# Two more products of constants per chunk in the relation passes of a graph network

## The reference, cut to what matters

```python
# second layer
t = jnp.einsum('nd,rdo->rno', h, weight)
msg = t[etype, src]
agg = jax.ops.segment_sum(msg, dst, num_segments=h.shape[0])
return jax.nn.relu(agg + bias)
# fourth layer
xt = jnp.einsum('ni,rio->rno', x, weight)
messages = xt[edge_type, col]
out = jax.ops.segment_sum(messages, row, num_segments=num_nodes)
return jax.nn.relu(out + bias)
```

## Time and profile before

| | us |
|---|---|
| median of 3 runs | 8551.53 (8549.6 to 8559.96) |
| the profiled execution | 8619.9 |
| first relation pass, 4015 to 5206 | 1191 |
| second relation pass, 7417 to 8582 | 1165 |
| PE busy over the whole execution | 4852.2 (56%) |
| POOL busy over the whole execution | 5243.4 (61%) |
| DVE busy over the whole execution | 3573.0 (41%) |

### The profile page before, as it was taken

One profiled execution on the slowest core, in us unless ns is written; L12 is line 12 of the kernel. 1 busy time (PEld: TensorE's weight loads), 2 busy tenths in 40 slices (PEclk: granted clock), 3 DMA queues, 4 the chain that ended last, 5 costly groups with the idle time before them and its releaser, 6 DMA issues. The chain is left out here.

```text
span 8619.9 us, 69117 instructions
## 1 busy us (share of the span) xinstructions
PE 4852.2 (56%) x17004; PEld 2990.1 (35%) x17004; DVE 3573.0 (41%) x9196; ACT 1730.7 (20%) x7055; POOL 5243.4 (61%) x5610
## 2 busy tenths in 40 slices
PE   3202235555557777777455543777777876655554
PEld 1100014444435555543333332222223663333332
DVE  4201014333335555564222224444445776244445
ACT  0000001111123333322000002222223874000000
POOL 5577756666666666632666662666665882366665
PEclk6655557777778888888666666878888998866666
DMA  3001012222235555554333335656666884333333
GB/s 96 2 3 39 15 40 90 90 89 89 91 116 176 177 175 175 177 114 156 92 93 93 92 93 67 186 184 187 187 187 177 267 271 156 117 93 92 91 94 85
DMA packets 422550, 1037.69 MB, mean 120 GB/s; under 512 B 159993, under 2 KB 188189, under 8 KB 415516
## 3 DMA queue, kind: packets, MB, share of 16 engines
q0 software_dynamic: 223616, 552.46, 22.9%
q1 hardware_dynamic: 198556, 480.95, 17.4%
HBM read 716.74 MB, written 316.30 MB: 120 GB/s over the span
## 5 line engine op out<-in xcount | busy, mean ns | idle before, releaser
L944 POOL DMA_INDIRECT rel_rows<-relation_rows,rel_ring_row x1640 | 1558.3, 950 | 1177.7 <-ACT rel_ring_end L937 695.1
L956 PE MATMUL rel_sums<-rel_rows,rel_hot 128*128 128x256 f32 x3280 | 1197.1, 509 | 1178.3 <-issue 448.5
L956 PEld LDWEIGHTS rel_sums<-rel_rows,rel_hot 128*128 128x128 f32 x3280 | 785.7, 252 | 1590.1 <-issue 1076.9
L982 DVE TENSOR_TENSOR g_acc<-rel_sums,g_acc 128x256 f32 x1224 | 517.8, 423 | 1532.9 <-DMA records_by_dst<-g_big 548.5
L1913 POOL DMA_INDIRECT nmax_rows<-messages,nmax_ring_row x832 | 788.6, 948 | 566.3 <-ACT nmax_ring_row L1869 327.6
L761 POOL DMA_INDIRECT rows_by_src<-spread_rows,spread_ring_place x832 | 803.2, 965 | 483.8 <-issue 254.3
L838 POOL DMA_INDIRECT both_rows<-batch_normed,both_ring_row x832 | 791.0, 951 | 460.9 <-ACT both_ring_end L807 231.3
L605 POOL DMA_INDIRECT records_by_dst<-sort_ring_rec,sort_ring_place x784 | 810.4, 1034 | 390.6 <-issue 241.2
L739 PE MATMUL spread_p_r<-g_big,spread_hot_t 128*128 x1664 | 631.5, 545 | 542.0 <-ACT spread_hot_t L674 358.8
L1961 DVE TENSOR_TENSOR g_big<-nmax_short,g_big 128x512 f32 x832 | 575.7, 692 | 659.9 <-PE nmax_short L1934 288.6
L1934 PE MATMUL nmax_short<-nmax_rows,g_ident_b 128*128 128x512 bf16 x2496 | 800.3, 436 | 0.0
(11 more groups left out here) (443 smaller groups left out, 6114.8 us busy)
## 6 DMA issues: line engine op xcount, KB each, us to landing
kept_rows<-nmax_rows SPq DMA_DIRECT2D x208, 536.0 KB
g_big<-kept_rows SPq DMA_DIRECT2D x208, 536.0 KB
both_out_rows<-rows_by_src SPq DMA_DIRECT2D x202, 520.0 KB
att_local_row<-local_of_edge SPq DMA_DIRECT2D x52, 512.0 KB
rel_rows<-relation_rows,rel_ring_row POOLq DMA_INDIRECT x1640
relation_rows<-mix_table SPq DMA_DIRECT2D x25, 1024.0 KB
relation_rows<-fin_table SPq DMA_DIRECT2D x25, 1024.0 KB, 3.9
rows_by_src<-spread_rows,spread_ring_place POOLq DMA_INDIRECT x832
```

Source lines behind the costliest of these rows:

```text
L944: pool.indirect_dma_start(rows[:, j, 0:words], None, table, bass.IndirectOffsetOnAxis(ap=ring_row[:, j:j + 1], axis=0)).then_inc(landed[n ...
L956: last = nc.tensor.matmul(sums[:, unit % slots, 0:width], hot[:, j, :], rows[:, j, :], start=of == 0, stop=of == GRAIN[k] - 1)
L982: nc.vector.tensor_tensor(at, sums[:, unit % slots, 0:width], at, ALU.add).then_inc(added, 1)
```

## The change

Behind each chunk's product PE computes two products of the constant `g.earlier` with itself, repeated four times to 512 columns, both bf16. They go to a PSUM bank of their own, `unused`, which nothing reads. To make room, `sums` gets 14 slots in seven banks instead of 16 in eight. The signal `summed` stays with the product of the group's fourth chunk.

```diff
-    ahead, slots = ring - 2, 16
+    ahead, slots, fills = ring - 2, 14, 2
...
-        sums = m.ps("sums", [P, slots, 8 * 512 // slots])
+        sums = m.ps("sums", [P, slots, 7 * 512 // slots])
+        unused = m.ps("unused", [P, GRP, P])
...
                     last = nc.tensor.matmul(sums[:, unit % slots, 0:width], hot[:, j, :], rows[:, j, :],
                                             start=of == 0, stop=of == GRAIN[k] - 1)
-                last.then_inc(summed, 1)
+                    if q == GRP - 1:
+                        last.then_inc(summed, 1)
+                    for _ in range(fills):
+                        nc.tensor.matmul(unused[:], g.earlier[:], g.earlier[:].unsqueeze(1).broadcast_to([P, GRP, P]),
+                                         start=True, stop=True)
```

## The result

The changed kernel takes 8597.99 us (median of 4 runs, 8592.52 to 8601.66) against 8553.39 for the kernel before (4 runs): ratio 1.0049, interval 1.0038 to 1.0061. It is slower by 45 us. The forecast was 354 us slower, so the sign and the place were right and the size was wrong by a factor of eight. The profiled execution takes 8599.9 us.

A forecast was written before the change was run, and what follows sets the result against it. The prediction took POOL's gathers, held up now and then waiting for ACT, as the bound. More stops (+350) and the signal's place (+4) made 354 on 8551.5, about 8905 us; own range 8740 to 9055, with rivals 8540 to 9420.

The forecast's parts named there:

- What bounds the kernel: Both relation passes: POOL's gathers, 1.254 us a chunk, plus 131 and 137 us of stops set the end; PE has room.
- The release in records: End of a late stretch: PE holds some 64 unsignalled loads and matmuls, so a release frees two groups instead of four.
- Cycles: From one POOL stop to the next: 4 groups, 16 chunks, so 52 and 50.5 stops instead of 23.4 and 24.5.
- The stop stays 5.6 us: POOL's stop at the end of each cycle keeps its length of 5.6 us net though stops come more often.
- the term of +306 to +387 us: Both passes: added POOL stops from twice the records, +306 with 4 groups a cycle, +387 with 3.5; 350 taken.
- The signal's place: End of each pass: summed has six fills of its group ahead of it, about 2 us per pass, +4 in all.
- One PSUM bank less: PE against DVE with 14 slots instead of 16: nothing taken; about +9 us if slots still bind.
- the hidden case: Rival, both passes: as many groups freed per stop as now, ring hides most; 0 to +90 us, 8550 to 8640; chance 0.22.
- PE bound by records: Rival, both passes: a late stretch comes each 160 records, 1.96 us a chunk, about 9410 us; chance 0.15.
- The faster case: Rival, both passes: fills shorten PE's idle time, signals stay prompt, POOL's stops return; 8285 to 8530 us; chance 0.13.

The follow-up runs named there:

- slots14_c: The kernel before with 14 PSUM slots instead of 16 and no fills, in conditions where POOL stops: ratio 1.0008 (0.9998 to 1.0018).
- pace2: The kernel before with a 128x300 write by POOL ahead of each gather, each waiting for the last, in conditions with stops: ratio 1.0136 (1.0119 to 1.0153).
- fill3: The changed kernel with three fills of 512 columns per chunk instead of two, in conditions with stops: ratio 1.0092 to the kernel before (1.0075 to 1.0109).
- change_again: The changed kernel as it is, run once more in conditions where POOL never stops: ratio 1.0004 to the kernel before (0.9995 to 1.0014).
- slots14_b: The kernel before with 14 PSUM slots instead of 16 and no fills, in conditions where POOL never stops: ratio 0.9999 (0.9989 to 1.0008).

## Why the prediction was wrong, step by step

- **What bounds the kernel: right, as far as it went.** POOL's gathers and its stops make up the pass, and PE has room: without stops 175 us of PE's time went into a pass and none showed, with stops 564 went into both passes and 45 showed. What the prediction did not see is that something other than POOL sets 1.42 us a chunk, which the stops only make up for.
- **The release in records: right for the change, but 64 is not a fixed number.** A release frees two groups with two fills, long or short, and one with six short ones, 64 loads and matmuls each. But it is 80 with three fills (two groups of 40), 48 in the second pass of slots14_c (three groups of 16), and in the first pass of before three of the 18 releases have a fifth group 0.23 us behind the fourth. In that second pass PE has a PSUM slot for each chunk, and four groups are just the 16 slots of before, three what fits in 14; so there the slots explain the release as well as the records. That PE holds a count of 64, as the prediction reads it, is not shown.
- **Cycles: nearly right, with some luck.** Forecast were 16 chunks and some 52 and 50 stops; measured were mostly 20 and mostly 16 chunks, and 43 and 53 stops (gaps of more than 1.6 us from one gather's start to the next). The way there was not sound: by the same count before had 33 and 26 stops and not the 23.4 and 24.5 from which the forecast set out.
- **The stop stays 5.6 us: this step failed,** and the prediction had named that as a sign of being wrong. In the cycles shown it is 3.1 to 3.8 us with two fills, 3.1 with three, 2.0 to 2.8 with six short ones. 5.6 / 32, 3.8 / 20, 3.1 / 16 and (2.0 + 2.8) / 20 are 0.175, 0.19, 0.19 and 0.24 us a chunk. I took the stop for a price that each cycle pays, and it is what POOL had run ahead since the last one: 1.42 less 1.25 us for each chunk, which is 0.17. Twice as many stops are then half as long, and the term of +306 to +387 us comes to +24 by the two profiles and to 33 to 39 by kernels in equal conditions. slots14_c (cycles of 28, stops of 4.9) and pace2 (no stop, and 117 us where step and stops make 390) show the same without fills. What sets the 1.42 us stays open. The rows had a warning: the earlier trace rows has 41 waits inside the first pass, 3.5 us each on the mean, and the earlier trace rows a stop of 4413.98 - 4407.93 - 1.25 = 4.8 us there and 5.6 in the second pass, and yet both passes came to 1.42 us a chunk. I divided the sum of the stops by 5.6 to get 23.4 of them, and so put in what I should have tested.
- **The signal's place: small, as forecast,** +4 in the sum. The ends of the passes grew by 8 and 6 us in the profile, but the second end was 25.6 us long in slots14_c, too, so the size of this part isn't shown.
- **One PSUM bank less: right in the time,** 1.0008 and 0.9999 for the slots alone. The slots do shorten the cycles of the second pass by one group where there are no fills; it costs nothing, as the stops shrink with them.
- **The rivals.** The time lies in the middle of the range of the hidden case, 8550 to 8640. The mechanism of that rival (as many groups freed as before) is not what happened: two are freed, and it costs little for another reason. PE bound by records wanted 1.96 us a chunk and fell with the change's own 1.437, and with the 1.448 of fill3. The faster case fell: fills do shorten PE's idle time and raise the clock, from 0.67 to 0.80, and from 0.76 to 0.98 in change_again, but the late stretches stayed where there were any, and the time did not fall. The Trainium skill, page "TensorE: Matmul & The Clock Gate", section "Why this matters for your kernels", advises to keep TensorE busy without gaps. The traces agree that the clock follows; the time does not, as PE doesn't set the pace of these passes.

## What to carry to other kernels

A producer that runs ahead and then stops may have a slower pace behind it, and the stops are only the balance: divide the whole stage by its steps before pricing one stop, and compare two stages whose stops have different lengths. Idle time of an engine that doesn't set the pace is nearly free (here the fills kept PE busy for 0.21 to 0.34 us more a chunk), and filling it for the sake of the clock is worth nothing unless that engine sets the pace. To test for such a floor, slow the producer on purpose: if the kernel loses less than the added time, something else was setting the pace.

## What the runs showed of the hardware

- The same kernel takes 8553 to 8610 us or 7627 to 7637, without a change in it. Nearly all of the difference lies in the six stages in which POOL issues indirect DMAs: in the profile of before they take 1123, 1237, 1250, 1182, 1225 and 1150 us from the first gather or scatter to the last, in that of slots14_b 1014, 1053, 1041, 1041, 1039 and 1012, together 967 of the 994 us between these two profiles. POOL's own step is the same in both (1.254 and 1.251 us in the passes).
- In the slower conditions there is a floor of 1.42 us for a chunk of 128 gathered rows. It held in kernels with 4 to 10 loads and matmuls a chunk within some 2% (1.418 to 1.448 us), whether POOL stopped 26 or 100 times a pass. It shows itself on other engines: PE starts an instruction per 1.40 us in late stretches and one per 0.70 us once POOL stands (4284.50, 4285.90, 4286.61 in the rows above), and ACT copies up to 41 us (36 in the changed kernel) after the start of PE's last matmul of the group that it waits for, where without stops, and in pace2, it does so after 0.4 to 0.7 us. The rows don't come late: in the middle of a pass the last DMA packet of a gather ends 2.4 us after the gather starts, with stops and without. Only behind the last gather of a pass it is more, in both conditions (12.5 and 8.2 us before, 13.7 and 8.0 in slots14_b). What resource has this pace isn't shown.
- Each further load or matmul that PE issues in a chunk raises that floor by 5 to 6 ns on the mean; with two fills it was the same at 128 and at 512 columns (1.0048 and 1.0049). Without stops 16 of them a chunk instead of 4 measured 1.0009 (1.0000 to 1.0019).
